# Attention's product with x as fp32r products over four tiles in turn, and its result turned back through DRAM

## The reference, cut to what matters

```python
xn  = (x - mean) / sqrt(var + EPS) * gamma + beta          # x was normalised once before
q, k, v = split(xn @ w_qkv);  q = q * 32 ** -0.5
k = softmax(k, axis=tokens)
context = einsum('bnhd,bnhe->bhde', k, v)                  # 4 heads of 32
out = einsum('bhde,bnhd->bnhe', context, q) @ w_out + b_out + (x normalised once)
x1  = x + layernorm(out)
for wg, wu, wd in experts:                                 # 8 of them, FFN = 512
    acc += (silu(xn1 @ wg) * (xn1 @ wu)) @ wd              # xn1 = layernorm(x1)
result = x1 + layernorm(acc)
```

## Time and profile before

| | |
|---|---|
| median of 3 runs | 547.96 us (547.76 to 548.49) |
| the profiled execution, its own time | 548.44 us |
| its span | 546.6 us |
| TensorE busy | 538.5 us, 99% |
| VectorE, ScalarE, POOL busy | 438.8, 344.4, 162.3 us |
| DMA | 25.52 MB, mean 47 GB/s |

### The profile page before, as it was taken

How to read it: one execution, slowest core, us unless ns; L and a number is a source line. 1 busy time by engine, 2 the same in 40 slices (tenths; PEclk the granted TensorE clock), 3 DMA queues, 4 the chain that set the end, 5 groups by cost and what they waited for, 6 DMA issues and landing times.

```text
span 546.6 us, 8678 instructions
## 1 busy us (share of the span) xinstructions
PE 538.5 (99%) x2627; PEld 466.0 (85%) x2627; DVE 438.8 (80%) x975; ACT 344.4 (63%) x625; POOL 162.3 (30%) x211
## 2 busy tenths in 40 slices
PE   8899999999999999999999999999999999999996
PEld 5688888888888888888888888888888888888885
DVE  6796986999768987798878898689976888778666
ACT  5886777556675566755657466665667555655554
POOL 5698670236003450043501244021620033001001
PEclk9999999999999999999999999999999999999999
DMA  6254110210101110101102011021010200010000
GB/s 200 76 162 129 57 59 1 77 59 17 43 37 41 58 35 25 60 18 59 58 1 77 29 33 58 1 77 47 13 40 0 78 20 20 19 40 0 21 0 20
DMA packets 29759, 25.52 MB, mean 47 GB/s; under 512 B 3217, under 2 KB 22417, under 8 KB 29713
## 3 DMA queue, kind: packets, MB, share of 16 engines
q1 hardware_dynamic: 28416, 24.33, 14.2%
q10 hardware_dynamic: 1296, 0.66, 0.4%
HBM read 15.80 MB, written 9.18 MB: 46 GB/s over the span
## 4 chain that ended last, share of the span: by engine, by line
PE 97%; DVE 1%; POOL 1%; issue 0%; POOLq 0%; ACT 0%; DVEq 0%; ACTq 0%
PE acc_att_ps L1136 10%; PE acc_att_ps L1139 10%; PE acc_att_ps L1137 10%; PE gate_ps L1136 10%; PE gate_ps L1139 10%; PE gate_ps L1137 10%; PE up_ps L1139 10%; PE up_ps L1136 10%; PE up_ps L1137 10%; PE acc_att_ps L1194 1%; PE acc_att_ps L1182 1%; PE up_ps L1240 1%; PE acc_att_ps L1170 0%; PE acc_att_ps L1190 0%; POOL rstd_x L575 0%
## 5 line engine op out<-in xcount | busy, mean ns | idle before, releaser
L687 ACT ACTIVATE gs<-gate_ps 128x512 f32<-128x512 f32 x255 | 152.1, 596 | 178.2 <-PE gate_ps L1139 175.7
L931 DVE TENSOR_TENSOR h<-gs,up_ps 128x512 f32<-128x512 f32 x231 | 157.9, 683 | 86.7 <-PE up_ps L1139 84.9
L918 DVE TENSOR_TENSOR h_lo<-h,h_hi 128x512 fp32r<-128x512 f32 x231 | 172.4, 746 | 0.1
L664 ACT ACTIVATE h_hi<-h 128x512 fp32r<-128x512 f32 x231 | 143.9, 623 | 7.5 <-DVE h L931 6.8
L1136 PE MATMUL gate_ps<-x1nT_hi,wg_hi 128*128 128x512 f32 (+1 forms) x254 | 98.5, 388 | 0.0
L1136 PE MATMUL acc_att_ps<-h_hi,wd_hi 128*128 128x512 f32 (+1 forms) x256 | 96.8, 378 | 0.0
L1137 PE MATMUL acc_att_ps<-h_hi,wd_lo 128*128 128x512 f32 (+1 forms) x256 | 96.8, 378 | 0.0
L1139 PE MATMUL acc_att_ps<-h_lo,wd_hi 128*128 128x512 f32 (+1 forms) x256 | 96.8, 378 | 0.0
L1139 PE MATMUL up_ps<-x1nT_lo,wu_hi 128*128 128x512 f32 (+1 forms) x254 | 96.1, 378 | 0.0
L1139 PE MATMUL gate_ps<-x1nT_lo,wg_hi 128*128 128x512 f32 (+1 forms) x254 | 96.1, 378 | 0.0
L1136 PE MATMUL up_ps<-x1nT_hi,wu_hi 128*128 128x512 f32 (+1 forms) x254 | 96.1, 378 | 0.0
(11 more groups left out here) (233 smaller groups left out, 531.6 us busy)
## 6 DMA issues: line engine op xcount, KB each, us to landing
w_raw<-in_L_ffn_Wg_dram SPq DMA_DIRECT2D x8, 256.0 KB, 3.3
w_raw<-in_L_ffn_Wu_dram SPq DMA_DIRECT2D x8, 256.0 KB, 3.0
w_raw<-in_L_ffn_Wd_dram SPq DMA_DIRECT2D x8, 256.0 KB, 3.0
x_in<-in_L_attn_x_dram SPq DMA_DIRECT2D x7, 256.0 KB, 2.8
t_dram_x1n<-t_blk_x1n SPq DMA_DIRECT2D x7, 256.0 KB, 2.0
t_out_x1n<-t_dram_x1n SPq DMA_DIRECT2D x28, 64.0 KB, 2.0
t_dram_acc<-t_blk_acc SPq DMA_DIRECT2D x7, 256.0 KB, 2.3
t_out_acc<-t_dram_acc SPq DMA_DIRECT2D x28, 64.0 KB, 2.0
```

Of the source, the lines that this page charges most:

```text
L664: act.activation(h_hi[s % NH][:, :], h_of(t, s)[:, :], ACT.Copy).then_inc(s_hhi, 1)
L687: act.activation(gs[q][:, :], gate_ps[q][:, :], ACT.Silu).then_inc(s_silu, 1)
L918: dve.tensor_tensor(h_lo[s % NH][:, :], h_of(t, s)[:, :], h_hi[s % NH][:, :].bitcast(F32), ALU.subtract).then_inc(s_hlo, 1)
L931: dve.tensor_tensor(h_of(t, s)[:, :], gs[q][:, :], up_ps[q][:, :], ALU.mult).then_inc(s_h, 1)
```

## The change

The product with x of batches 2 to 7 becomes three fp32r matmuls of 512 columns with G as weights, in high and low halves, and the halves of xnT, which the key product already uses, as moving operand. They read four tiles in turn (`in_turn`), and so does the key product now. This leaves the result with channels on the partitions and tokens along the free axis, so it is turned: a block transpose from PSUM (`z_T`), a store to DRAM and four loads, and the sum z reads what came back. G's halves are ACT's copy (now fp32r) and a subtraction on DVE (`G`, new there), and the product waits for both. The block tile is shared with E, and the buffer of what comes back is zn's, with the waits for that. exp puts the four-way order of the keys back by reading its bank with a stride of four. The tables move the steps behind.

```diff
 MIDDLE = ("acc",)
-FRONT = ("xnT", "kmax", "E", "A", "M", "G", "z", "x1n_hi", "x1n_lo")
+FRONT = ("xnT", "kmax", "E", "A", "M", "G", "z_T", "z", "x1n_hi", "x1n_lo")
 FIRST_PE = {"A": 11, "M": 13, "G": 15, "attn": 16}
 FIRST_DVE = {"E_T": 4, "next_stats": 8, "A": 12, "M": 14, "z": 17, "z_stats": 17, "next_T": 19, "wk_lo": 20,
              "x1_stats": 21, "x1n_T": 25, "next_xnT_lo": 28, "x1n_lo": 31}
 FIRST_ACT = {"E_store": 5, "E_load": 8, "G": 16, "wk_hi": 18, "next_xnT": 26, "next_xnT_hi": 27, "x1n_hi": 30}
 FIRST_POOL = {"y": 2, "yb": 6, "next_rstd": 10, "next_xn": 13, "z_rstd": 18, "x1": 18, "x1_rstd": 22}
 PE_AT = {"kT": 1, "A": 9, "M": 11, "G": 13, "attn": 14}
-DVE_AT = {"kmax": 2, "acc": 2, "E_T": 3, "next_stats": 6, "A": 10, "fin_stats": 10, "M": 12, "fin_scale": 12, "next_T": 14,
-          "z": 15, "z_stats": 15, "x1_stats": 20, "next_xnT_lo": 22, "x1n_T": 23, "x1n_lo": 29}
-ACT_AT = {"exp": 2, "G": 14, "next_xnT": 20, "next_xnT_hi": 21, "x1n_hi": 28}
-POOL_AT = {"yb": 4, "next_rstd": 7, "next_xn": 10, "fin_rstd": 11, "fin_out": 13, "z_rstd": 16, "x1": 16, "x1_rstd": 20}
+DVE_AT = {"kmax": 2, "acc": 2, "E_T": 3, "next_stats": 6, "A": 10, "fin_stats": 10, "M": 12, "fin_scale": 12, "G": 14,
+          "z_T": 15, "next_T": 16, "z": 18, "z_stats": 18, "x1_stats": 22, "next_xnT_lo": 23, "x1n_T": 25, "x1n_lo": 30}
+ACT_AT = {"exp": 2, "G": 14, "next_xnT": 21, "next_xnT_hi": 22, "x1n_hi": 29}
+POOL_AT = {"yb": 4, "next_rstd": 7, "next_xn": 10, "fin_rstd": 11, "fin_out": 15, "z_rstd": 19, "x1": 19, "x1_rstd": 22}
 BUSY = {"start": 7, "w": 1, "U": 3, "z": 2, "xn": 2, "attn": 1, "x1n": 2}
...
 def pairs(v):
     return v.rearrange("p (a b) -> p b a", a=2)
+def in_turn(v):
+    return v.rearrange("p (j q) -> p q j", j=4)
 def pairs_of(v, i):
...
         A_sb = sb("A_sb", [P, D])
         M_sb = sb("M_sb", [P, D])
         G_sb = sb("G_sb", [P, D])
+        G_hi = sb("G_hi", [P, D], F32R)
+        G_lo = sb("G_lo", [P, D], F32R)
         z = sb("z", [P, J, D])
         zn = sb("zn", [P, J, D])
         x1 = [sb(f"x1_{i}", [P, J, D]) for i in range(2)]
...
         turned = ("x", "E", "x1n", "acc")
         t_blk = {k: sb(f"t_blk_{k}", [P, N]) for k in turned}
         t_out = {k: sb(f"t_out_{k}", [P, N]) for k in turned}
-        t_dram = {k: nc.dram_tensor(f"t_dram_{k}", [P, N], F32) for k in turned}
+        t_blk["z"] = t_blk["E"]
+        t_out["z"] = zn[:, :, :].rearrange("p j d -> p (j d)")
+        t_dram = {k: nc.dram_tensor(f"t_dram_{k}", [P, N], F32) for k in (*turned, "z")}
         fn = sb("fn", [P, J, D])
         res = sb("res", [P, J, D])
...
                     if not last:
                         load_blocks("E", b + 1)
                     load_blocks("acc", b)
+                if not first and not last:
+                    store_blocks("z", s_z_blk, b)
+                    sp.wait_ge(s_x1, b)
+                    load_blocks("z", b)
+                if nxt:
+                    store_blocks("x", s_xh_blk, b + 1)
+                if not first:
                     store(b - 1)
                 if nxt:
-                    store_blocks("x", s_xh_blk, b + 1)
                     load_blocks("x", b + 1)
                 if not last:
                     store_blocks("x1n", s_x1n_blk, b + 1)
...
                     act.activation(xnT_hi[:, :], xnT[:, :], ACT.Copy).then_inc(s_xnT_hi, 1)
                 if at == "exp":
                     act.wait_ge(s_kmax, c)
-                    act.activation(ET[:, :], att_ps[:, :], ACT.Exp, bias=kmax_neg[:, 0:1], scale=1.0,
-                                   accum_out=esum[:, 0:1]).then_inc(s_ET, 1)
+                    if first:
+                        act.activation(ET[:, :], att_ps[:, :], ACT.Exp, bias=kmax_neg[:, 0:1], scale=1.0,
+                                       accum_out=esum[:, 0:1]).then_inc(s_ET, 1)
+                    else:
+                        act.activation(ET[:, :].rearrange("p (j q) -> p j q", j=J),
+                                       att_ps[:, :].rearrange("p (q j) -> p j q", j=J), ACT.Exp, bias=kmax_neg[:, 0:1],
+                                       scale=1.0, accum_out=esum[:, 0:1]).then_inc(s_ET, 1)
                 if at == "E_store":
                     act.wait_ge(s_E_blk, c)
...
                         act.dma_start(dst, src).then_inc(s_t_load["E"], 16)
                 if at == "G":
                     act.wait_ge(s_G_ps, c)
-                    act.activation(G_sb[:, :], att_ps[:, 0:D], ACT.Copy).then_inc(s_G, 1)
+                    act.activation(G_sb[:, :] if first else G_hi[:, :], att_ps[:, 0:D], ACT.Copy).then_inc(s_G, 1)
                 if at == "x1n_hi":
                     act.wait_ge(s_t_load["x1n"], c * 64)
                     act.activation(plain(x1nT_hi[par][:, :]), from_group(t_out["x1n"][:, :]),
...
                     dve.wait_ge(s_M_ps, c)
                     dve.scalar_tensor_tensor(out=M_sb[:, :], in0=att_ps[:, 0:D], scalar=erec[:, 0:1],
                                              in1=R_sb[:, :], op0=ALU.mult, op1=ALU.add).then_inc(s_M, 1)
+                if at == "G":
+                    dve.wait_ge(s_G, c)
+                    dve.tensor_tensor(G_lo[:, :], att_ps[:, 0:D], G_hi[:, :].bitcast(F32),
+                                      ALU.subtract).then_inc(s_G_lo, 1)
+                if at == "z_T":
+                    dve.wait_ge(s_attn_ps, c)
+                    dve.wait_ge(s_t_store["E"], c * 16)
+                    dve.transpose(grouped(t_blk["z"][:, :]), by_group_of_acc(att_ps[:, :])).then_inc(s_z_blk, 1)
                 if at == "z":
                     dve.wait_ge(s_yb, c)
-                    dve.wait_ge(s_attn_ps, c)
-                    dve.tensor_tensor(z[:, :, :], att_v, yb[:, :, :], ALU.add).then_inc(s_z, 1)
+                    if first:
+                        dve.wait_ge(s_attn_ps, c)
+                        dve.tensor_tensor(z[:, :, :], att_v, yb[:, :, :], ALU.add).then_inc(s_z, 1)
+                    else:
+                        dve.wait_ge(s_t_load["z"], (c - 1) * 64)
+                        dve.tensor_tensor(z[:, :, :].rearrange("p j (i r) -> p j i r", r=32), from_group(t_out["z"][:, :]),
+                                          yb[:, :, :].rearrange("p j (i r) -> p j i r", r=32), ALU.add).then_inc(s_z, 1)
                 if at == "z_stats":
                     dve.wait_ge(s_z, c)
                     stats_of("z", c, z)
...
                                   by_group(xh[:, :, :].rearrange("p j d -> p (j d)"))).then_inc(s_xh_blk, 1)
                 if at == "E_T":
                     dve.wait_ge(s_ET, c)
+                    if c > 2:
+                        dve.wait_ge(s_t_store["z"], (c - 2) * 16)
                     dve.transpose(grouped(t_blk["E"][:, :]), by_group(ET[:, :])).then_inc(s_E_blk, 1)
                 if at == "x1n_T":
                     dve.wait_ge(s_x1n, c)
...
             def attention(at, c, first):
                 if at == "kT":
                     pe.wait_ge(s_xnT_hi, c - 1)
-                    products(att_ps[:, :], wk_hi[:, :], wk_lo[:, :], xnT_hi[:, :], xnT_lo[:, :], True, True, s_xnT_lo,
-                             c - 1).then_inc(s_kT_ps, 1)
+                    products(att_ps[:, :], wk_hi[:, :], wk_lo[:, :], in_turn(xnT_hi[:, :]), in_turn(xnT_lo[:, :]), True,
+                             True, s_xnT_lo, c - 1).then_inc(s_kT_ps, 1)
                 if at == "A":
                     pe.wait_ge(s_t_load["E"], c * 64)
...
                 if at == "G":
                     pe.wait_ge(s_M, c)
                     pe.matmul(att_ps[:, 0:D], wqT[:, :], M_sb[:, :], start=True, stop=True).then_inc(s_G_ps, 1)
-                if at == "attn":
+                if at == "attn" and not first:
+                    pe.wait_ge(s_G, c)
+                    pe.wait_ge(s_G_lo, c - 1)
+                    products(att_ps[:, :], G_hi[:, :], G_lo[:, :], in_turn(xnT_hi[:, :]), in_turn(xnT_lo[:, :]), True,
+                             True, s_xnT_lo, c - 1).then_inc(s_attn_ps, 1)
+                elif at == "attn":
                     pe.wait_ge(s_G, c)
                     for j in range(J):
                         last = pe.matmul(att_ps[:, j * D:j * D + D], xnT[:, j * P:j * P + P], G_sb[:, :],
```

More of the change, by code:

```diff
@@ L270, in build @@
         s_G = sem("s_G")
+        s_G_lo = sem("s_G_lo")
         s_attn_ps = sem("s_attn_ps")
@@ L341, in build @@
         s_E_blk = sem("s_E_blk")
+        s_z_blk = sem("s_z_blk")
         s_x1n_blk = sem("s_x1n_blk")
-        s_t_store = {k: sem(f"s_t_store_{k}") for k in turned}
-        s_t_load = {k: sem(f"s_t_load_{k}") for k in turned}
+        s_t_store = {k: sem(f"s_t_store_{k}") for k in (*turned, "z")}
+        s_t_load = {k: sem(f"s_t_load_{k}") for k in (*turned, "z")}
         s_fn = sem("s_fn")
```

## The result

The changed kernel takes 549.70 us (median of 7 runs, 549.03 to 551.21), the kernel before, on the same chip, 548.21 (547.76 to 548.57). The ratio is 1.0035, 95% interval 1.0025 to 1.0045: slower by 1.5 us, where the forecast was 1.35 us faster. The span grew from 546.6 to 548.5 us. Single runs scatter over 2.2 us, where those of the kernel before scatter over 0.8. One run of a later experiment (e1) took 1464 us; its ratio goes without it, and nothing here shows a cause.

What follows compares the result with a forecast made beforehand. TensorE, busy 99% of the span, was taken to bound the kernel. The terms -1.47 - 0.36 + 0.48 sum to -1.35 us, with the DRAM trips hidden, giving 546.6 us; range 545.9 to 547.7.

Steps and rivals of the forecast that it cites:

- Part 2: Key product: three products at 0.216 us, 0.65 instead of 0.71; gain 0.06 us, six times: 0.36 us.
- part 1: x product of batches 2 to 7: three products replace eight f32 passes; gain 0.245 us, six times: 1.47 us.
- The bounds: Pace of the new products: 0.216 us at the fast end, plain 0.236 at the slow, or further off f32's 0.405.
- rival (d): Key and x products: four tiles in turn much slower, pace over 0.254; at 0.405, +5.5 us, 553.4; chance 0.07.
- Part 3: x product waits for G_lo on VectorE, behind an h_lo slowed by POOL's res; loss 0.08 us, six times: 0.48.
- Part 4: Way back through DRAM: trips of z and x1n hidden, cover 1.8 us for z, 1.6 for x1n's low half.
- a good microsecond: ScalarE's wait for x1n's trip, asked for at 143.3 and ending about 144.5, with silu of step 29 behind.
- 6.1 us in all: Length of x's own trip through DRAM, store issue to landed loads; also taken for the trips of z and x1n.
- Rival (e): z's or x1n's trip outlasts its cover, beyond 1.8 us over 6.1; one microsecond beyond gives +4.6; chance 0.05.

Runs made afterwards that it cites:

- e1: The changed kernel with the key product, and exp with it, reading its columns plainly again: 548.87 us, ratio 1.001 to the kernel before.
- e3: The changed kernel with key and x products reading two tiles in turn, 1 KB apart: 547.21 us, ratio 0.9981 to the kernel before.
- e9: The changed kernel with two neighbouring tiles read in turn and fin_scale in step 11 instead of 12: 546.15 us, ratio 0.9964 to the kernel before.
- e10: The changed kernel with fin_scale on VectorE in step 11 instead of 12, alone: 548.77 us, ratio 1.0014 to the kernel before.

## Why the prediction was wrong

**Part 2, and with it part 1: wrong, and this decided the sign.** The step that failed was the pace of the new products: "I take 0.216, as the two readings are alike in hopping between tiles at every column and differ only in how many". How many is what counts: two 0.216, four 0.277. Over 36 products this is 36 x 0.061 = 2.2 us, more than the whole gain that was forecast, and e1 to e3 gave it back in portions (0.83, 1.64 and 2.5 us against the changed kernel). The bounds had the value between plain and f32 passes, and rival (d) named the very threshold, a pace over 0.254, with a chance of 0.07. That chance was too low: nothing in the trace read four tiles, and one step of a pattern (plain to two) is no ground for the next.

**The page's rule.** The Trainium skill, "SBUF — State Buffer", section "Door 1: The DMA port swizzle" (full speed within a 16-byte line, a penalty at each new one), was put aside because the pair was faster than the plain reading. For pairs it fails here (0.216 against 0.236), and for every second and every fourth column and for many places it is right in kind (0.42 to 0.50). Four tiles in turn leave the line at every column as every fourth column does, and are slower than the plain reading, but by far less (0.277). The row that contradicted it had two places only, and was used to judge four.

**Part 3: mechanism right, size off.** The collision with res, the unmoved order of POOL, the place and the 0.28 us of G_lo were as written; the loss was 0.13 us a batch instead of 0.08. The sum began the first x product about 0.08 late and let the others follow at their pace; it began 0.05 late, and the second lost another 0.08. e9 and e10 gave the 0.13 back.

**Part 4: the usual case right, the unusual one missed.** z started at 123.18 (forecast 123.2), in part by luck: z_T was 0.35 later than in the sum and z's trip 0.45 shorter (5.65 us). VectorE came later too, so that it waited 0.06 us at most in the six batches, where half a microsecond was forecast. ScalarE's wait of "a good microsecond" was 1.03 to 1.23. The exp with its stride takes 0.69 us as before, so its "nothing" was right. But "6.1 us in all" was read from one trip, the slowest of x's six; most of these trips take 5.3 to 5.7, and in the changed kernel one of x1n's took 6.94 and one of x's 6.72. Rival (e) priced the excess for all six batches or none; it came in one, 0.49 us, and beyond 1.5 us of excess instead of 1.8 (2.6 less the usual wait of 1.1).

**The account.** -1.35 (forecast), +2.2 (reading), +0.3 (G_lo, 6 x 0.05), +0.5 (landing) = +1.65 us, against +1.8 in the spans and +1.5 in the medians.

## What to carry to other kernels

Before a tensor is read in a new order by TensorE, measure that order: the pace of an fp32r product ran from 0.216 to about 0.50 us by it alone, and the best was two places in turn. A subtraction that a product waits for should not stand behind an instruction that POOL can hold up; and for an engine without work of its own the numbers in its list move nothing, only the order does (here fin_out, from 13 to 15). And a chain that goes through DRAM three times needs slack for a landing 2 us late at each trip, since slack moved between them only moves the stall.

## What had not been expected of the hardware

Reading two places in turn is faster than reading straight on (0.216 against 0.236 us for 512 columns), with 512 bytes or 1 KB between them; 128 bytes apart they took 0.24, as the pair 512 bytes apart did in the same place. Reading every second column (0.42) is nearly as slow as reading every fourth (0.46). A 64 KB load or a 256 KB store that usually lands in 2 us took 3.6 and 4.4 where both instruction queues fetched at the same time, and none of 1547 such landings without a fetch took over 2.54.
